# Expert tiles of four, two and one seat in place of tiles of two

## The reference

```python
t = _to_tokens(x)                                  # 2 x 4096 tokens x 128
logits = ln(t) @ Wr.T + br                         # 8 experts
w, idx = top_k(softmax(logits), 2)                 # two experts per token
h = gelu(einsum('nd,edf->enf', ln(t), W1) + b1)    # 128 -> 512
y = einsum('enf,efd->end', h, W2) + b2             # 512 -> 128
t = t + einsum('ne,end->nd', combine, y)           # weights of the two chosen experts
```

## Time and profile before

| | |
|---|---|
| median of the runs | 989.05 us (987.12 to 992.66) |
| profiled execution, span from first to last instruction | 1121.3 us |
| profiled execution's own time | the page gives no other time than the span |
| TensorE matmul / weight load busy | 810.7 / 683.7 us |
| GpSimd busy | 616.5 us |
| VectorE busy | 565.6 us |
| ScalarE busy | 516.3 us |
| indirect DMAs, gathers and scatters | 284 and 284 |
| mean granted TensorE clock | 0.844 of full speed |

### The profile page before, as it was taken

One profiled execution on the slowest core, in us unless ns is written; L12 is line 12 of the kernel. 1 busy time (PEld: TensorE's weight loads), 2 busy tenths in 40 slices (PEclk: granted clock), 3 DMA queues, 4 the chain that ended last, 5 costly groups with the idle time before them and its releaser, 6 DMA issues.

```text
span 1121.3 us, 14549 instructions
## 1 busy us (share of the span) xinstructions
PE 810.7 (72%) x4233; PEld 683.7 (61%) x4233; DVE 565.6 (50%) x1308; ACT 516.3 (46%) x1407; POOL 616.5 (55%) x590
## 2 busy tenths in 40 slices
PE   1854389897867867986689488975996677796780
PEld 0434268785767655864678376854786565674670
DVE  8957902280500291999775296999681003300005
ACT  1405045562444445653266156643393443453563
POOL 1000266676655675788623755888646466665640
PEclk9876579997988888998589689998798788998895
DMA  8001344453565742553137733543256446555456
GB/s 317 1 0 57 123 149 125 139 156 98 174 193 187 248 156 87 172 158 118 38 109 236 254 110 109 183 138 102 65 162 220 135 128 201 194 157 174 133 162 225
DMA packets 54557, 165.23 MB, mean 147 GB/s; under 512 B 13632, under 2 KB 13645, under 8 KB 54224
## 3 DMA queue, kind: packets, MB, share of 16 engines
q1 hardware_dynamic: 36304, 128.87, 34.6%
q0 software_dynamic: 18176, 35.44, 10.8%
HBM read 134.89 MB, written 31.20 MB: 148 GB/s over the span
## 4 chain that ended last, share of the span: by engine, by line
PE 40%; DVE 26%; ACT 10%; another core or an unknown queue 10%; issue 8%; DMA 3%; POOL 2%; SPq 0%; POOLq 0%; ACTq 0%; DVEq 0%
PE h_ps L783 14%; PE yT_ps L796 12%; DVE state L1302 6%; DVE work L1288 4%; DVE work L1283 4%; ACT hT L596 4%; PE turn_ps L718 4%; PE acc_ps L735 3%; DVE tok L1252 2%; PE acc_ps L755 2%; DVE work L1296 2%; PE xT_ps L772 2%; ACT yT L607 1%; PE h_ps L886 1%
## 5 line engine op out<-in xcount | busy, mean ns | idle before, releaser
L511 POOL DMA_INDIRECT xg<-xn_rows,tile_rows x284 | 305.4, 1075 | 243.1 <-DVEq L1218 126.6
L520 POOL DMA_INDIRECT y_rows<-yr,tile_rows x284 | 306.9, 1080 | 236.1 <-ACT yr L616 147.5
L783 PE MATMUL h_ps<-xT,expert 128*128 128x256 f32 (+1 forms) x1376 | 317.7, 381 | 64.9 <-ACT hT L596 37.7
L796 PE MATMUL yT_ps<-hT,expert 128*128 128x256 f32 (+1 forms) x1376 | 300.2, 369 | 34.9 <-ACT yT L607 21.6
L596 ACT ACTIVATE hT<-h_ps,expert 128x256 f32<-128x256 f32 (+1 forms) x688 | 250.7, 451 | 154.7 <-PE h_ps L783 70.0
L783 PEld LDWEIGHTS h_ps<-xT,expert 128*128 128x128 f32 x1376 | 244.4, 213 | 103.1 <-issue 52.6
L796 PEld LDWEIGHTS yT_ps<-hT,expert 128*128 128x128 f32 x1376 | 247.5, 209 | 71.6 <-ACT yT L607 26.1
L1252 DVE SCALAR_TENSOR_TENSOR tok<-work,share,tok 128x128 f32<-128x128 f32 x224 | 61.2, 346 | 340.3 <-DMA work<-y_rows 336.9
L607 ACT ACTIVATE yT<-yT_ps,expert 128x256 f32<-128x256 f32 (+1 forms) x172 | 72.9, 444 | 170.3 <-PE yT_ps L796 92.4
L584 ACT ACTIVATE xT<-xT_ps 128x256 f32<-128x256 f32 x144 | 56.4, 392 | 117.8 <-PE xT_ps L772 59.7
L772 PE MATMUL xT_ps<-ident,xg 128*128 128x128 f32 x284 | 61.2, 298 | 58.2 <-DMA xg<-xn_rows,tile_rows 45.4
(11 more groups left out here) (210 smaller groups left out, 661.1 us busy)
## 6 DMA issues: line engine op xcount, KB each, us to landing
expert<-in_experts SPq DMA_DIRECT2D x172, 514.5 KB
work<-y_rows SPq DMA_DIRECT2D x24, 512.0 KB
xn_rows<-work SPq DMA_DIRECT2D x16, 512.0 KB, 4.4
xg<-xn_rows,tile_rows POOLq DMA_INDIRECT x284
y_rows<-yr,tile_rows POOLq DMA_INDIRECT x284
tok<-in_x_tokens SPq DMA_DIRECT2D x8, 512.0 KB, 6.9
state<-in_x SPq DMA_DIRECT2D x2, 2048.0 KB, 17.1
work<-y_rows SPq DMA_DIRECT2D x16, 256.0 KB, 6.1
```

The lines of the kernel that those rows point to most:

```text
L511: pool.indirect_dma_start(xg[:, s, h, :], None, xn_rows[unit], bass.IndirectOffsetOnAxis(ap=tile_rows[unit % 2][:, at, 0, h:h + 1], axis=0)) \
L520: pool.indirect_dma_start(y_rows[unit], bass.IndirectOffsetOnAxis(ap=tile_rows[unit % 2][:, at, 1, h:h + 1], axis=0), yr[:, s, h, :], None ...
L783: mm = pe.matmul(h_ps[c // 2][:, c % 2, cols], expert[:, t.load(h) % W_RING, c * P:(c + 1) * P], xT[:, t.slot(2), cols], start=True, stop= ...
L796: mm = pe.matmul(yT_ps[:, cols], expert[:, t.load(h, d) % W_RING, HIDDEN + c * P:HIDDEN + (c + 1) * P], hT[:, s, c, cols], start=(c == 0), ...
```

## The change

A tile now has up to 512 slots. Each expert's seats are split by the bits of its seat count: as many groups of four as fit, then a pair, then a single. A unit has ten tiles of four seats (quads), eight of two (doubles) and 15 single seats in eight tiles: 26 tiles, 33 weight loads, 71 seats as before. Two of the doubles come first (EARLY), then the quads, the other doubles, the singles. Where experts have more groups of four than ten, the rest lies in two doubles each.

- Gathers and scatters go by granules of two seats (36 a unit); rings of six granules; the gather of granule g + LAG (11) stands ahead of the scatter of granule g; between the runs six granules are gathered (G_FIRST) ahead of the last three scatters (BORDER).
- The hidden banks: a quad's chunk fills one of the two banks of 512 columns, a double's two chunks fill one. The activated hidden has a ring of six such fills (H_RING), and each fill has its own signal that the down-products have used it.
- `place_in_tiles` takes the positions of `WHEN` as granule numbers and gives the tile and place.
- VectorE's seat arithmetic works with three classes in place of two.
- The one-hot lanes lie in `work[1]` (in `tok[1]` for unit 0) in place of `shared` and `hT`.

```diff
-SLOTS = 256
-HALVES = SLOTS // P
+PAIR, QUAD = 2, 4
+SLOTS = QUAD * P
+SEATING = ([(FIRST_DOUBLE + PAIR * i, PAIR, 1) for i in range(EARLY)]
+           + [(QUAD * i, QUAD, 1) for i in range(QUADS)]
+           + [(FIRST_DOUBLE + PAIR * i, PAIR, 1) for i in range(EARLY, DOUBLES)]
+           + [(seat, min(PAIR, SEATS - seat), min(PAIR, SEATS - seat)) for seat in range(FIRST_SINGLE, SEATS, PAIR)])
+TILES = len(SEATING)
+GRANULES = -(-SEATS // PAIR)
-RING = 5
+X_RING, Y_RING, H_RING = 6, 6, 6
-G_AHEAD = 5
-S_BEHIND = 3
-G_FIRST = 2
+LAG = 11
+G_FIRST = X_RING
+BORDER = 3
...
+def place_in_tiles(at):
+    if at >= GRANULES:
+        return round(TILES + at - GRANULES, 1)
+    j = next(j for j in range(TILES) if at < GRANULE_AT[j + 1])
+    part = (at - GRANULE_AT[j]) / (GRANULE_AT[j + 1] - GRANULE_AT[j])
+    return round(j + (0 if part < AFTER_UP / 2 else AFTER_UP if part < (AFTER_UP + AFTER_DOWN) / 2 else AFTER_DOWN), 1)
...
+            def gather(g):
+                unit = g // GRANULES
+                if g >= X_RING:
+                    pool.wait_ge(s_xt_ps, g - X_RING + 1)
+                for h, seat in enumerate(seats_of_granule(g)):
+                    pool.indirect_dma_start(xg[:, g % X_RING, h, :], None, xn_rows[unit],
...
+            for run in RUNS:
+                first, end = run[0] * GRANULES, (run[-1] + 1) * GRANULES
+                if run[0] == 0:
+                    lists_ready(0)
+                    for g in range(G_FIRST):
+                        gather(g)
+                for g in range(first + G_FIRST, first + LAG):
+                    gather(g)
+                for g in range(first, end):
+                    if g + LAG < end:
+                        if (g + LAG) % GRANULES == 0:
+                            lists_ready((g + LAG) // GRANULES)
+                        gather(g + LAG)
+                    if g == end - BORDER and run[-1] + 1 < UNITS:
+                        lists_ready(run[-1] + 1)
+                        for ahead in range(end, end + G_FIRST):
+                            gather(ahead)
+                    scatter(g)
...
             def up(t):
                 pe.wait_ge(s_xt_sb, t.done())
...
+                first, fills = t.fills()
+                each = CHUNKS // fills
                 for c in range(CHUNKS):
-                    if c % 2 == 0 and t.old(-1):
-                        pe.wait_ge(s_h_sb, t.done(-1, 2, c // 2 + 1))
+                    fill = first + c // each
+                    if c % each == 0 and fill >= 2:
+                        pe.wait_ge(s_h_sb, fill - 1)
...
-                op(dve.tensor_scalar(n_tiles_i[:], n_tiles_i[:], SLOTS.bit_length() - 1, None, ALU.logical_shift_right))
-                op(dve.tensor_scalar(whole, n_tiles_i[:], float(HALVES), None, ALU.mult))
+                for i, bits in enumerate((P - QUAD, PAIR, 1)):
+                    op(dve.tensor_scalar(seats_i[:, 1 + i, :], seats_i[:, 0, :], bits, None, ALU.bitwise_and))
```

More of the change, by code:

```diff
@@ L109, in wait, with running, fills_of @@
         self.eng.wait_ge(self.sem, self.n - back)
+def running(counts):
+    return [sum(counts[:i]) for i in range(len(counts) + 1)]
+def fills_of(seats):
+    return CHUNKS if seats == QUAD else CHUNKS // 2
+LOAD_AT = running([loads for _, _, loads in SEATING])
+GRANULE_AT = running([-(-seats // PAIR) for _, seats, _ in SEATING])
+FILL_AT = running([fills_of(seats) for _, seats, _ in SEATING])
 class Tile:
@@ L129, in drains, with done, seats, granules @@
         return self.last <= self.s <= self.last + 1
[L131 to L132 removed]
+    def done(self, d=0):
+        return self.s + d + 1
     def slot(self, n, d=0):
         return (self.s + d) % n
[L137 to L146, removed]
+    def seats(self, d=0):
+        return SEATING[self.at(d)[1]][1]
     def parts(self, d=0):
[L150 removed]
+        return SEATING[self.at(d)[1]][2]
     def load(self, h=0, d=0):
         unit, at = self.at(d)
[L155 removed]
+        return unit * LOADS + LOAD_AT[at] + h
+    def granules(self, d=0):
+        unit, at = self.at(d)
+        return range(unit * GRANULES + GRANULE_AT[at], unit * GRANULES + GRANULE_AT[at + 1])
+    def fills(self, d=0):
+        unit, at = self.at(d)
+        return unit * FILL_AT[-1] + FILL_AT[at], FILL_AT[at + 1] - FILL_AT[at]
+def tile_of_granule(g):
+    unit, i = divmod(g, GRANULES)
+    return unit * TILES + next(j for j in range(TILES) if i < GRANULE_AT[j + 1])
+def seats_of_granule(g):
+    unit, i = divmod(g, GRANULES)
+    j = next(j for j in range(TILES) if i < GRANULE_AT[j + 1])
+    seat, seats, _ = SEATING[j]
+    first = PAIR * (i - GRANULE_AT[j])
+    return range(seat + first, seat + min(first + PAIR, seats))
+def landed(g, ring):
+    return 16 * sum(len(seats_of_granule(i)) for i in range(g % ring, g + 1, ring))
 def columns(t, d=0):
     n = t.parts(d)
[L161 removed]
+    size = t.seats(d) * P // n
     return [(h, slice(h * size, (h + 1) * size)) for h in range(n)]
@@ L194, in plan @@
     found = {}
-    for at, name, *args in WHEN[u]:
+    for at, name, *args in sorted(WHEN[u], key=lambda step: step[0]):
         if name in work:
-            at = round(at, 1)
+            at = place_in_tiles(at)
             before = found.get(at)
@@ L525, in begin, with lists_ready @@
-            def begin(u, ahead):
+                                            bass.IndirectOffsetOnAxis(ap=tile_rows[unit % 2][:, 1, seat:seat + 1], axis=0),
+                                            yr[:, g % Y_RING, h, :], None, bounds_check=PAIRS - 1, oob_is_err=False) \
+                        .then_inc(s_scat[g % Y_RING], 16)
+            def lists_ready(u):
                 pool.wait_ge(s_rows, u + 1)
                 pool.wait_ge(s_xn_st[u], 16 * QUARTERS)
-                for d in ahead:
-                    gather(Tile(u, 0), d)
@@ L602, in copy_y @@
                 s = t.slot(2, d)
-                act.wait_ge(s_y_ps, t.done(d))
+                act.wait_ge(s_h_used, sum(t.fills(d)))
                 if t.old(d - 2):
```

257 lines of the change are left out of this document (125 added, 132 removed).

## The result

The changed kernel takes 1032.53 us (median of 4 runs, 1027.36 to 1036.74) against 990.86 us (4 runs, 987.12 to 992.71) for the kernel before: ratio 1.0423, 95% interval 1.038 to 1.0466. It is slower, as forecast, but by 41.7 us where the sum said 25.6, and the time lies 5.5 us above the range.

What follows compares the result with a forecast made beforehand. The prediction took GpSimd's indirect DMAs (1.30 us each) to bound units 0 and 3, VectorE units 1 and 2. Its terms, 10.4 + 7.4 + 7.8 + 2 + 1 - 3 = +25.6 on 989.05, gave about 1015 us, range 968 to 1027.

Steps and rivals of the forecast that it cites:

- the sum: All terms of the change added: +25.6 us on 989.05, about 1015 us.
- item 1: Wide tiles on TensorE: time goes by columns, 1.3 us to spare per two seats; value 0.
- Items 1 and 2: Wide tiles on TensorE, and 33 expert loads for 43: value 0 each, the loads up to 3 us.
- The step about TensorE: Matmul time already goes by columns, so 512 columns give at most 0.1 us a quad.
- Item 3(a): End of unit 0: last scatter behind 164 indirect DMAs, not 156; +10.4 us, bounds +2.6 to +12.5.
- Item 3(b): Unit 1 to 2: eight more gathers ahead of five scatters, +10.4 less 3 of cover; +7.4 us, bounds 0.5 to 10.4.
- Item 3(c): Unit 2 to 3: 21 scatters left behind the first gather, not 15; +7.8 us, bounds 0 to 9.4.
- Item 4: More seat arithmetic on VectorE: +2 us at route 0, +1 for routes 2 and 3 together.
- Item 5: Positions of routes and mixing steps among the tiles: routes stay, mixing steps fall on quads; value 0.
- Item 6: Six ring slots and the longer lag let GpSimd work on while others stall: -3 us granted, at most 12.
- Item 7: TensorE's clock: quads make gaps fewer and longer, a half-speed start costs less than the gap; value 0.
- the worst case: Rival: GpSimd is the bound and nothing covers, full penalties; +38, 1027 us, chance 0.13.

Runs made afterwards that it cites:

- before_order11: Kernel before with only the change's order of gathers and scatters on GpSimd (LAG 11, five tiles gathered first), old tiles and 43 loads: 1031.95 us, ratio 1.0427.
- before_lag11: Kernel before with the lag of 11 alone, two gathers first at unit 2's lists as before: 1022.45 us, ratio 1.0276.
- after_borders: Changed kernel with another order of gathers and scatters at the borders between units only, LAG 11 kept inside units: 1011.89 us, ratio 1.0174.
- before_extra_iota: Kernel before with one more GpSimd instruction, an iota, ahead of each tile's gathers in units 0 and 3: 1017.92 us, ratio 1.0246.

## Why the prediction was right in sign and too low

- **What bounds the kernel.** Right for unit 3: GpSimd starts an indirect DMA every 1.30 us and never idles beyond its 0.30 us of issue, 157 in 202.4 us before and 163 in 210.3 us after. The Trainium skill ("Perfetto Trace Analysis", What "DMA-bound" means) calls a kernel bound by its DMA sequencer when the issuing engine's track is solid with DMA slices, the slices being descriptor generation; the trace agrees in unit 3, with 0.99 us busy and 0.30 of issue for each, and the added iotas showed that the time follows. In unit 0 it is only two thirds true: GpSimd idled 3.0 us before and 7.5 after, and TensorE has little of the 1.3 us to spare that item 1 gave it, since it is busy 188 of 209 us (before, unit 0):

```profile
132.00:341.00 209.00, 188.26 (x1090) 166.50 (x1091) 62.99 (x174) 123.06 (x334) 158.69 (x156) 0.94 0.59 189
```

- **Items 1 and 2, wide tiles and fewer loads, value 0.** Right in sum, since before_order11 and after agree within 1 us, but this is partly luck, as the table below shows. The step about TensorE holds: it is as busy as before with fewer instructions (windows of unit 2's mixing, before, then after):

```profile
607.00:763.00 156.00, 133.71 (x713) 116.27 (x712) 140.92 (x206) 89.08 (x234) 110.47 (x91) 0.89 0.44 134
```

```profile
632.00:789.00 157.00, 134.32 (x589) 92.53 (x589) 143.22 (x211) 80.07 (x179) 106.19 (x89) 0.87 0.34 107
```

- **Item 3(a), +10.4.** The count held (164th, not 156th), the size did not. From the first gather to the last scatter of unit 0 it took 14.9 us more, beyond the upper bound of 12.5: 10.4 for the eight DMAs and 4.5 of new idle time. Old tiles in the same order took 11.7 (before_order11) and 12.1 (before_lag11), so most of the excess, about 3 us, came with the wide tiles. GpSimd waits there for the first quads' results, and ScalarE, which copies them, waits from 150 to 206 us only for TensorE. Here are three of its waits in after:

```profile
180.84 0.99 POOL L576 DMA_INDIRECT y_rows<-yr,tile_rows  x1 [4.64 <-ACT yr L673]
193.80 1.00 POOL L576 DMA_INDIRECT y_rows<-yr,tile_rows  x1 [2.93 <-ACT yr L673]
205.32 1.00 POOL L576 DMA_INDIRECT y_rows<-yr,tile_rows  x1 [0.90 <-ACT yr L673]
```

- **Item 3(b), +7.4.** The 3 us of cover were a reading of the stalled profile: undisturbed, the gap reduction waits 1.5 us, and no profile shows less, so nothing is left to cover with. The profiles show 10.0 us, near the upper bound of 10.4; taking the gathers back gave 7.3.
- **Item 3(c), +7.8.** Right: 7.8 from first gather to last scatter, 7.4 from the lists.
- **Item 4, seat arithmetic.** At route 0 it is 1.7 for 2 in this pair of profiles. Over all the undisturbed ones the first gather comes at 130.9 to 132.1 us with the old arithmetic and at 133.8 to 136.1 with the new, so 2 to 3 us is the better figure. Of routes 2 and 3 nothing can be told apart.
- **Item 5, positions, 0.** Wrong by 2.1 us in after (a wait of 3.65 for 1.55): the turned tokens come late. In after_borders the same waits are longer by 6.8 and 5.7 us, but there the order of the gathers is in them too.
- **Item 6, deeper rings, -3.** The failed step. I took the sixth slots and the longer lag for a relief of GpSimd's waits for results and granted 3 us. The waits grew. In unit 0 GpSimd idles 7.5 us for 3.0, and unit 3 had none to relieve. So this term is +4.5 and not -3. Old tiles with the lag of 11 idle 5.5 us in unit 0, there at gathers that wait for TensorE to turn rows; the quads of after idle at scatters. So some 2.5 of the 4.5 us come with the longer lag also without quads. A second cost of the lag, ScalarE's waits for room among the results, I had not bounded either. With old tiles it is shown and costs 7.4 us in unit 2. In after ScalarE waits 79.3 us, 30 times, for scatters to land (215.6 us, 76 times, in before_order11), but its stages grow by no more there than the other terms account for (+0.6 us in unit 2's mixing, +7.4 in unit 3 for 7.8 counted). So the record does not show that it made after late.
- **Item 7, the clock, 0.** Not tested by itself. The mean granted clock is 0.889 before, 0.872 after and 0.886 in before_order11, whose profile is 2.7 us shorter than that of after. TensorE's matmuls are busy 759.7, 773.6 and 775.0 us.
- **The sum.** In the profiles +33.5 was measured for 25.6. The 7.5 us of item 6 nearly make up the difference. Item 3(b)'s 2.6 and item 5's 2.1 come on top, 3 us that unit 1's mixing and routing took less go against them, and of item 4 about 1 does not show. Medians and profiles differ by another 8 us, 5.2 of after and 2.7 of before, by which profiled executions lie off their medians; I can't assign them to a place. Without these 8 us the time would lie inside the range. The range ended at 1027 because the worst case was a sum of the same counted terms.

By stages, in us of the profiled executions. A row runs from the mark of the row above to its own (scatters by their start); the columns behind "before takes" are differences to it:

| up to | before takes | after | before_order11 | before_lag11 | after_borders |
|---|---|---|---|---|---|
| first gather | 132.1 | +1.7 | -1.1 | -0.7 | +4.0 |
| last scatter of unit 0 | 208.7 | +14.9 | +11.7 | +12.1 | +5.7 |
| gap reduction, unit 1 | 45.7 | +2.0 | -0.4 | -0.3 | +6.5 |
| lists of unit 2 | 158.0 | -3.1 | -3.1 | +3.7 | -1.6 |
| last scatter of unit 1 | 16.2 | +10.0 | +7.5 | 0.0 | -4.9 |
| gap reduction, unit 2 | 45.4 | -0.2 | +0.1 | +0.3 | +7.8 |
| lists of unit 3 | 156.0 | +0.6 | +8.9 | +7.4 | +0.8 |
| last scatter of unit 3 | 205.3 | +7.4 | +7.4 | +6.8 | +2.8 |
| end | 24.4 | +0.1 | -0.2 | +0.3 | -0.5 |
| sum | 991.8 | +33.5 | +30.8 | +29.5 | +20.7 |

One line of it is not safe to read. Up to the lists of unit 2, before_order11 and before_lag11 run the same instructions, and yet they take 154.9 and 161.7 us from the gap reduction to those lists. So some 7 us there can be the spread of single executions, and the -3.1 of after can't be told from it.

The totals of after and before_order11 agree by different ways. The old tiles in the new order pay 8.9 us in unit 2, where the turned tokens stand behind a full ring of results. The changed kernel pays about as much in a later first gather, a slower unit 0, a longer wait at the gap reduction and one more granule gathered between the runs. That the sums meet is luck. So the value 0 of items 1 and 2 is not shown by it.

## What to carry to other kernels

When an in-order queue is the bound, count what stands ahead of the instruction that others wait for. A larger look-ahead is paid at every border between stages; it can also be paid in the result ring that is emptied later, and at the start of a stage. Fit the look-ahead to the stage: long inside, short at its end, and put finished stores into the wait for the next stage's inputs, as far as they end before those inputs come. Before trusting stalls of unknown origin in a profile, compare its span with the timed runs; here 130 us of them were one execution's own, and even the slack read from beside them (9.87 us, 1.5 undisturbed) was wrong. And when two kernels take the same time, compare them stage by stage before you say that what differs between them costs nothing.

## What the runs showed of the hardware

- An iota of 512 bf16 columns takes 592 ns as one run of 512 and 1200 ns as a pattern of 128 by 4 with step 0 inside, on the same engine and size. The second is a single instruction at the start of the kernel (1196 ns in before's second profile). The pattern is the difference I see between the two; it was not tested by itself:

```profile
L515 POOL IOTA extra<- 128x512 bf16 x72 | 42.6, 592 | 134.7 <-DVEq L1227 134.6
L495 POOL IOTA lane<- 128x512 bf16 x1 | 1.2, 1200 | 0.0
```

- The DMA behind such an iota starts 0.16 us after the iota's end, where 0.30 us lie between two DMAs; the iota itself starts with no gap behind a DMA (254.11 in before_extra_iota).
- The time of a 32-bit product still goes by its columns at 512: eight records of 512 columns take 3.60 us in after, eight of 256 columns 1.89.

```profile
207.70 3.60 PE L861 MATMUL yT_ps<-hT,expert 128*128 128x512 f32 x8
```

- An indirect DMA of 128 rows of 512 bytes keeps GpSimd busy 0.99 us on average in unit 3 of before and of after, and the next starts 1.30 us after it.
